# Turning the exponents of two cross attentions by products with diagonals of the inverse sums

## The reference

```python
kv_rope = kv_c * cos[None] + _rotate_half(kv_c) * sin[None]
q_r = jnp.einsum('bshq,hqr->bhsr', q_big, W_qr)
k_r = jnp.einsum('bld,hdr->bhlr', kv_rope, W_kr)
scores = jnp.einsum('bhsr,bhlr->bhsl', q_r, k_r)
attn = jax.nn.softmax(scores, axis=-1)
ctx_c = jnp.einsum('bhsl,bld->bhsd', attn, kv_rope)
ctx_lat = jnp.einsum('bhsd,hkd->bshk', ctx_c, w_kc_kv)
out = ctx_lat.reshape(b, s, H * K) @ Wo.T
```

## Time and profile before

| | |
|---|---|
| median of 3 runs | 2045.65 us (2041.42 to 2046.24) |
| profiled execution | 2043.4 us, span of its instructions 2041.6 us |
| mean granted PE clock | 0.981 |
| PE busy | 1916.4 us (94%), 9274 instructions |
| VectorE busy | 1308.6 us (64%), 2881 instructions |
| ScalarE busy | 919.8 us (45%), 2258 instructions |
| GpSimd busy | 1016.8 us (50%), 926 instructions |
| loop over batches in L0x | about 130 to 360 us |
| loop over batches in L1x | about 1102 to 1334 us |

### The profile page before, as it was taken

The page is one execution under the profiler, slowest core; times in us unless marked ns, Lnnn a source line. Parts: engine busy times, 40 slices in busy tenths (PEclk is TensorE's granted clock), DMA queues, the critical chain, the costliest instruction groups (busy, mean ns, idle before and its releaser), DMA issues. The chain is left out here.

```text
span 2041.6 us, 30196 instructions
## 1 busy us (share of the span) xinstructions
PE 1916.4 (94%) x9274; PEld 1432.8 (70%) x9274; DVE 1308.6 (64%) x2881; ACT 919.8 (45%) x2258; POOL 1016.8 (50%) x926
## 2 busy tenths in 40 slices
PE   7988999999999999999997899989997999999996
PEld 6857999886588844577674799977764666566664
DVE  4578887466651122477776788858865666677665
ACT  2555555233412100244444555535434665666662
POOL 1248885112252200377777788667402455566662
PEclk9999999999999999999999999999996999999998
DMA  5551332200211100012225133320035999999997
GB/s 184 201 202 55 109 106 67 84 1 1 104 61 42 43 8 0 20 61 85 94 81 193 52 104 100 109 70 1 15 130 186 311 338 328 248 233 237 233 237 195
DMA packets 104957, 251.55 MB, mean 123 GB/s; under 512 B 14800, under 2 KB 40912, under 8 KB 96304
## 3 DMA queue, kind: packets, MB, share of 16 engines
q1 hardware_dynamic: 82224, 196.02, 29.0%
q0 software_dynamic: 21136, 51.11, 10.8%
q10 hardware_dynamic: 1440, 2.49, 0.3%
HBM read 279.44 MB, written 55.07 MB: 164 GB/s over the span
## 5 line engine op out<-in xcount | busy, mean ns | idle before, releaser
L99 PE MATMUL banks<-L1f_w,L1f_xT 128*128 x760 | 263.2, 490 | 0.9 <-ACT L1f_xT L2781 0.9
L2999 POOL DMA_INDIRECT moe_sums<-L1f_y,L1f_row x94 | 149.6, 1592 | 171.6 <-DVE L1f_is_who L2868 93.0
L99 PEld LDWEIGHTS banks<-L1f_w,L1f_xT 128*128 128x128 f32 x760 | 138.1, 192 | 78.1 <-issue 3.3
L160 POOL TENSOR_TENSOR rstd<-rstd,power 128x1 f32<-128x1 f32 x48 | 32.0, 666 | 221.8 <-DVE rstd L154 221.8
L3007 POOL DMA_INDIRECT L1f_xg<-moe_rows,L1f_row x95 | 107.9, 1136 | 60.3 <-DVE L1f_spare L2859 25.2
L99 PE MATMUL banks<-L0f_down,L0f_z 128*128 128x512 f32 x256 | 111.1, 592 | 1.5 <-DVE L0f_z L2241 1.5
L2702 PE MATMUL banks<-L1f_w,L1f_zT 128*128 x190 | 98.3, 599 | 4.6 <-DVE L1f_z_rest L2839 4.6
L99 PE MATMUL banks<-L0f_hT_hi,L0f_ug_hi 128*128 128x512 f32 x256 | 100.0, 391 | 0.0
L99 PE MATMUL banks<-L0f_hT_lo,L0f_ug_hi 128*128 128x512 f32 x256 | 99.6, 389 | 0.0
L99 PE MATMUL banks<-L0f_hT_hi,L0f_ug_lo 128*128 128x512 f32 x256 | 99.6, 389 | 0.0
L2313 POOL TENSOR_TENSOR L0f_ug_lo<-w,L0f_ug_hi 128x512 fp32r<-128x512 f32 x32 | 42.9, 1353 | 113.1 <-ACT L0f_ug_hi L2217 113.1
(11 more groups left out here) (439 smaller groups left out, 5893.5 us busy)
## 6 DMA issues: line engine op xcount, KB each, us to landing
L1f_w<-in_experts SPq DMA_DIRECT2D x95, 1280.0 KB
L1f_laid<-moe_counts SPq DMA_DIRECT2D x59, 512.0 KB, 6.3
w<-in_L1x_heads SPq DMA_DIRECT2D x16, 704.0 KB, 4.0
L0x_q<-L0x_far SPq DMA_DIRECT2D x20, 512.0 KB
L1x_q<-L1x_far SPq DMA_DIRECT2D x20, 512.0 KB
w<-in_L0x_heads SPq DMA_DIRECT2D x8, 1216.0 KB, 6.2
L0x_far<-L0x_away_far SPq DMA_DIRECT2D x8, 1024.0 KB
w<-in_wug SPq DMA_DIRECT2D x8, 1024.0 KB, 4.9
```

What stands on the lines that cost most here:

```text
L99: ins = pe.e.matmul(out, w, m, start=first and n == 0, stop=last and n == len(pairs) - 1)
L160: pool.e.tensor_tensor(self.rstd[:, i:i + 1], self.rstd[:, i:i + 1], self.power[:, 0:1], ALU.pow).then_inc(self.rstd_set.sem, 1)
L2999: pool.e.indirect_dma_start(self.sums[j % 2][:, :], bass.IndirectOffsetOnAxis(ap=self.row[:, j:j + 1], axis=0), self.y[j % self.NY][:], No ...
```

## The change

VectorE no longer multiplies the exponents by the inverse sums; it adds the tail to the sums and takes the inverse (`invert`). ScalarE makes four diagonal matrices from the identity for each batch, one for each group of 128 queries, by a copy with the inverse sums as a scale per partition (`spread_shares`), and puts them side by side into one of the `xn` buffers. PE multiplies the exponents, as the stationary operand as before, by these diagonals instead of transposing them by the identity; the result, turned and weighed, goes to the same banks. The waits follow: PE waits for the four diagonals (`diagonal`), ScalarE for the inverse (`inverted`) and for the turn of two batches before.

```diff
--- before.py
+++ after.py
@@ -288,7 +288,7 @@
         self.scored = take("scored", 2 * B)
         self.peak = take("peak", 3 * B)
         self.exped = take("exped", 5 * B)
-        self.weighed = take("weighed", 3 * B)
+        self.inverted, self.diagonal = take("weighed", 2 * B), take("masked", 4 * B)
         self.prob_turned = take("prob_turned", 2 * B)
         self.pT_hi = take("pT_hi", 2 * B)
         self.pT_lo = take("pT_lo", 2 * B)
@@ -538,13 +538,14 @@
         src = self.prob[b % 3]
         if b == 0:
             self.folds_kept(pe, self.FIRST)
-        pe.wait_ge(self.weighed, 3 * b + 3)
+        pe.wait_ge(self.diagonal, 4 * b + 4)
         pe.wait_ge(self.pT_hi, 2 * b)
         pe.wait_ge(self.pT_lo, 2 * b)
+        shares = self.shares(b)
         for c in range(LC):
             for r in range(4):
-                ins = pe.e.transpose(self.t_bank[:, c * BANK + r * P:c * BANK + (r + 1) * P], src[:, r, c * P:(c + 1) * P],
-                                     self.sh.ident[:])
+                ins = pe.e.matmul(self.t_bank[:, c * BANK + r * P:c * BANK + (r + 1) * P], src[:, r, c * P:(c + 1) * P],
+                                  shares[:, r * P:(r + 1) * P], start=True, stop=True)
             ins.then_inc(self.prob_turned.sem, 1)
 
     def mix(self, pe, b):
@@ -582,6 +583,8 @@
                 self.exponent(act, b)
             if self.FIRST + b < XH:
                 self.keep_folded(act, self.FIRST + b, self.o_bank)
+            if 0 <= b - 1 < B:
+                self.spread_shares(act, b - 1)
             t = b - self.LAG_TURN
             if 0 <= t < B:
                 for c in range(LC):
@@ -593,6 +596,19 @@
             o = b - self.LAG_VALUES - BPT + 1
             if o > self.LAST and o < self.LAST + BPT:
                 self.after.halves_hi(act, o - self.LAST - 1)
+
+    def shares(self, b):
+
+        return self.sh.xn[b % 3]
+
+    def spread_shares(self, act, b):
+
+        act.wait_ge(self.inverted, 2 * b + 2)
+        act.wait_ge(self.prob_turned, 2 * (b - 2))
+        rec = self.small[b % 4][:, 4, :]
+        for r in range(4):
+            act.e.activation(self.shares(b)[:, r * P:(r + 1) * P], self.sh.ident[:], ACT.Copy,
+                             scale=rec[:, r:r + 1]).then_inc(self.diagonal.sem, 1)
 
     def keep_context(self, act, b):
         act.wait_ge(self.mixed, b + 1)
@@ -639,7 +655,7 @@
             if b < B:
                 self.find_peak(dve, b)
             if 0 <= b - 1 < B:
-                self.weigh(dve, b - 1)
+                self.invert(dve, b - 1)
             if 0 <= t < B:
                 for c in range(LC):
                     hi, lo = cut(self.pT, slice(None), c)
@@ -680,21 +696,19 @@
         for g in range(2):
             bank = self.s_bank[(2 * b + g) % 3]
             dve.wait_ge(self.scored, 2 * b + g + 1)
-            dve.wait_ge(self.weighed, 3 * (b - 3))
+            dve.wait_ge(self.inverted, 2 * (b - 3))
             dve.e.tensor_reduce(mx[:, 2 * g:2 * g + 2], bank.rearrange("p (r n) -> p r n", r=2), AX_X,
                                 ALU.max).then_inc(self.peak.sem, 1)
         dve.wait_ge(self.peak, 3 * b + 2)
         dve.e.tensor_scalar(neg, mx, -1.0, 0.0, ALU.mult, ALU.min).then_inc(self.peak.sem, 1)
 
-    def weigh(self, dve, b):
-        dst, (sums, tail, rec) = self.prob[b % 3], (self.small[b % 4][:, n, :] for n in (2, 3, 4))
+    def invert(self, dve, b):
+        sums, tail, rec = (self.small[b % 4][:, n, :] for n in (2, 3, 4))
         dve.wait_ge(self.exped, 5 * b + 5)
-        dve.e.tensor_tensor(sums, sums, tail, ALU.add).then_inc(self.weighed.sem, 1)
-        dve.wait_ge(self.weighed, 3 * b + 1)
-        dve.e.reciprocal(rec, sums).then_inc(self.weighed.sem, 1)
-        dve.wait_ge(self.weighed, 3 * b + 2)
-        dve.e.tensor_tensor(dst[:], dst[:], rec.rearrange("p (r o) -> p r o", o=1).to_broadcast([P, 4, LC * P]),
-                            ALU.mult).then_inc(self.weighed.sem, 1)
+        dve.e.tensor_tensor(sums, sums, tail, ALU.add).then_inc(self.inverted.sem, 1)
+        dve.wait_ge(self.inverted, 2 * b + 1)
+        dve.wait_ge(self.diagonal, 4 * (b - 3))
+        dve.e.reciprocal(rec, sums).then_inc(self.inverted.sem, 1)
 
 
 class FoldedQueries(LatentAttention):
```

## The result

The changed kernel takes 2116.35 us (median of 4 runs, 2111.07 to 2121.68), the kernel before, run beside it, 2043.54 us (2037.44 to 2046.24): a ratio of 1.0357, interval 1.0332 to 1.0381. That is 72.8 us more; the forecast was 61 more, 2106 us. The profiled execution took 2111.07 us. All of it is in the two loops over batches. From the start of the first exponent to the last record of the last turn they take 225.6 and 227.5 us before, 263.4 and 262.8 after, 73.0 us more together. The rest of the span is 5 us shorter; between the profiled executions of these experiments it differs by up to 11 us, so the loops are the better measure.

The account below looks back on a forecast made before the run. PE was taken to bound each cross attention after its opening iterations, which the ring paces. Products 23.8 us plus activations 6.7 made 30.5 per stage, 61.0 for two, giving 2106 us; range 2092 to 2124.

Parts of the forecast that it names:

- the likeliest case: The sum of the forecast's own terms, 2106 us, with its own range of 2096 to 2113; chance 0.81.
- the rival in which ScalarE becomes the bound: Cross attentions: activations over 0.40 us make the ring set the period; at 0.44 us each, 2124 us; chance 0.08.
- That rival's sign: PE idle behind the diagonals or the context's low half, with a batch period over 7.9 us.
- Weighing worth nothing: Both cross attentions: removing VectorE's 64 weighing instructions, 79 us of its work, was costed as no gain.
- Products, 0.88 us a batch: PE's turns: eight real products for eight transposes, 8 more records per batch, paid in 27 batches, 23.8 us per stage.
- The rival of fourfold products: PE's turns: real products take four times the transposes, 2.37 us more per batch; 2187 us; chance 0.03.
- Activations, 0.28 us each, 1.12 a batch: Four ScalarE activations per batch lengthen each of iterations 1 to 6 by the whole 1.12 us, 6.7 us per stage.
- In the start: Opening iterations of each cross attention, where PE waits for the ring: exponents 7.34 us apart, forecast about 8.5.
- I add nothing: PE's clock, which falls in a cross attention's opening iterations, may fall once more or less there; costed at nothing.
- In the body the diagonals are hidden, with 0.46 us to spare: After the opening iterations the ring grows to 7.38 us, under PE's new 7.84, so the activations cost nothing.
- the ring: Per-batch loop of ScalarE and VectorE without PE: exponents, copies, low halves, peaks; 6.26 us without folded weights.
- No added wait: PE's wait for ScalarE's diagonals and ScalarE's wait for the inverse were forecast to cost nothing.

Follow-up runs that it names:

- the products alone: The kernel before, with the eight turns made real fp32 products with the identity, VectorE's weighing kept and no diagonals: 2092.35 us, ratio 1.0247.
- the update late: The changed kernel, with VectorE's residual sum and statistics of a finished tile moved behind the peaks of the next iteration: 2104.17 us, ratio 1.0309.
- the run with the reduction: The changed kernel, with the peaks negated and clamped by one tensor_reduce over maxima written beside zeros: 2107.48 us, ratio 1.0317.

## Why the prediction was right, and where it was not

The direction and the larger part of the size were right. The time is 10 us over the forecast: inside the range, above the likeliest case's own end of 2113. The range reached that far only for the rival in which ScalarE becomes the bound because an activation takes 0.44 us. It took 0.295, so that the range holds is in part luck. That rival's sign did come, PE idle behind the context's low half, but in one iteration of four and for another reason (step 4).

1. *Weighing worth nothing*: right. Without it the kernel takes 0.9985 of its time, and the loops are no shorter.

2. *Products, 0.88 us a batch*: right in price (1.70 - 0.79 = 0.91; the period 6.96 to 7.87 in the run with the products alone), somewhat high in number: that run's loops are 22.9 and 20.8 us longer, which is 24 turns of 0.91 on the mean, not 27. The rival of fourfold products is out. The Trainium skill (TensorE: Matmul & The Clock Gate, section Terms), for FP32, gives the transpose mode as 4 times faster. That does not hold here: two records of 0.106 us stand for one of 0.099, 1.70 us for 0.79, a factor of 2.15.

3. *Activations, 0.28 us each, 1.12 a batch*: 0.295 and 1.18. In the start the exponents come 8.48 us apart, forecast 8.5. From the first exponent to the eighth it is 7.1 us more in the first loop and 6.1 in the second, forecast 6.7. The run with the update late shows the start's cost together with its aftermath: 17.9 us more in both loops than with the products alone, forecast 13.4. Two turns behind the start, 8.87 and 8.15 us after the one before in the first loop, are a part of it, and there the clock is in it, which the prediction put at nothing ("I add nothing"): PE waits 2.46 us before 183.38, and its granted clock is 0.66 from 182 to 186 us:

```profile
182.00:186.00 4.00, 2.62 (x6) 2.15 (x7) 3.82 (x10) 1.05 (x4) 0.00 (x0) 0.66 0.00 0
```

With the products alone it is 1.00 in the same stretch. No run separates how much of the 4.5 us is the clock's.

4. *In the body the diagonals are hidden, with 0.46 us to spare*: this is the step that failed. "In the first iteration without folded weights the ring takes 6.26 us ... So the ring has 0.70 us to spare in the body." The 6.26 was one ring, of the first iteration of the body, before any tile was finished. Without the update the ring's length is as forecast (7.40, forecast 7.38). The iteration that carries VectorE's update takes 9.63. The ring's mean, if nothing else held it, is (9.63 + 3 x 7.40) / 4 = 7.96, over PE's 7.87. Even a mean below that does not hide it: after the update the ring gains 0.47 us on PE in each of two iterations, and the third takes 7.88, since it waits for what PE makes of the next keys, here ScalarE's copy of them:

```profile
270.17 0.37 ACT L625 CAST L0x_kT_hi<-banks 128x256 fp32r<-128x256 f32 x1 [0.78 <-PE banks L521]
```

So the ring can have 0.93 in hand, and an iteration of 9.63 makes PE late by 9.63 - 7.87 - 0.93 = 0.83, the 8.70 measured. By the same count the run with the reduction, 9.13, must be late by 0.33, and 8.22 was measured, although its mean of 7.83 is under 7.87. Five such turns in a loop, and one at the end (8.70, where the run with the update late has 6.95), are 5 x 0.83 + 1.75 = 5.9 us; 11.8 for both. The loops of the change are 11.4 us longer than that run's, its median 12.2. The trace of before had the sign of it: the exponents there are 7.98 us apart across an update (of which the second row is a part) and 6.25 behind it. Their mean, (7.98 + 3 x 6.25) / 4 = 6.68, stays under 6.96, but it says nothing of what the fourth iteration needs once the ring grows.

```profile
227.16 0.47 ACT L624 ACTIVATE L0x_prob<-banks,L0x_small 128x256 f32<-128x256 f32 x1 [2.00 <-DVE L0x_small L687]
231.56 0.68 DVE L657 TENSOR_TENSOR x<-x,banks 128x512 f32<-128x512 f32 x1
235.14 0.48 ACT L624 ACTIVATE L0x_prob<-banks,L0x_small 128x256 f32<-128x256 f32 x1 [3.03 <-DVE L0x_small L687]
241.39 0.47 ACT L624 ACTIVATE L0x_prob<-banks,L0x_small 128x256 f32<-128x256 f32 x1 [2.32 <-DVE L0x_small L687]
```

5. *No added wait*: right but for 1.2 us, once in the loop of L0x. (The 7.4 us that the prediction calls PE's longest wait are the total of six; the longest is 2.2.)

By the loops the sum is 43.7 (products) + 17.9 (diagonals, start) + 11.4 (diagonals, body) = 73.0 us; the forecast had 47.6 + 13.4 + 0. The first two errors, 3.9 too much and 4.5 too little, nearly cancel; the body's 11.4 is what is left.

## What to carry to other kernels

A slack taken from one iteration of a ring is not the loop's: look for the iteration that carries what is done only now and then, and ask how far the ring can run ahead before it, since the mean alone does not decide. Work added to two engines that hold each other costs what the slower path costs, not the sum: measure each alone before either is blamed. By the loops, the same four instructions cost 29 us inside the ring and 6 behind the last copy that another engine waits for: most of the price is the place.

## What the runs showed of the hardware

I had not expected that a VectorE instruction of 128x4 could wait for GpSimd. In the changed kernel's two loops the negation of the peaks took 0.17 us in 49 of 64 cases; 44 of these met no instruction of GpSimd, and five began in the last 0.12 us of one. It took 0.56 to 0.68 in the 14 that began earlier inside a tensor_tensor of GpSimd, and 0.33 in one that began inside a cast; all 15 ended within 0.03 us of it. As a scalar_tensor_tensor with two operands in SBUF it took up to 0.67. As a reduction, with one operand, it took 0.16 in all 16 cases that began inside a tensor_tensor, and the two-operand addition behind it was held instead (0.28 to 0.79). The price is not the instruction's own size but what is left of the other's.

It goes the other way as well. In the kernel before, 25 of GpSimd's 64 casts of the keys began while VectorE was inside the weighing; they took 1.06 to 1.39 us and ended 0.26 us behind it, while the other 39 took 0.39 to 0.41. Without the weighing all 64 took 0.39 to 0.41. With the change GpSimd's busy time falls by 47.7 us at the same number of instructions; as the run without the weighing has no shorter loops, that was worth no time.

The Trainium skill says, in SBUF — State Buffer, section SBUF: two separate sides, that VectorE and GpSimd share a pair of ports as an exclusive lock, which whichever starts first has for its whole instruction: a GpSimd instruction, or a VectorE one in a 2-port mode or with two SBUF inputs (the latter only against a GpSimd instruction that reads SBUF). The runs agree with it for the instructions with two SBUF inputs, which were held, and for the reduction, which was not (0.16 us in 16 of 16). That the tensor_scalar form runs in a 2-port mode no run here shows; it was held in the 15 cases above.
